# Audio-tower kernel: the instruction lists of all engines laid out anew, pair-2 convolution taps and weight centring moved to TensorE

## The reference, cut to what matters

```python
x_sp = depthwise conv over tokens, 3 taps, padding 1, + conv_b
h    = x_sp.T @ lin_w.T + lin_b + emb.mean(0)          # 250 x 128
h    = layernorm(h) * ln_g + ln_b
n    = layernorm(h)
QK   = (n Wq) (n Wk)^T                                 # 250 x 250
c0   = argmin(row sums of QK of batch 0)
A    = softmax(QK / 8), row c0 set to zero
h    = h + A (n Wv)
n    = layernorm(h)
h    = h + tril(W2) gelu(tril(W1) n + b1) + b2         # along the 128 features
```

## Time and profile before

| what | value |
|---|---|
| time, median of three runs | 105.33 us (104.79 to 105.63) |
| the profiled execution: its own time | 105.14 us |
| the profiled execution: its span, first to last instruction | 102.7 us |
| busy share of the span | TensorE 88%, VectorE 74%, ScalarE 69%, GpSimd 45% |
| granted TensorE clock, mean | 0.996 |

### The profile page before, as it was taken

The page is one execution under the profiler, slowest core; times in us unless marked ns, Lnnn a source line. Parts: engine busy times, 40 slices in busy tenths (PEclk is TensorE's granted clock), DMA queues, the critical chain, the costliest instruction groups (busy, mean ns, idle before and its releaser), DMA issues.

```text
span 102.7 us, 1986 instructions
## 1 busy us (share of the span) xinstructions
PE 90.9 (88%) x568; PEld 74.5 (73%) x568; DVE 76.2 (74%) x297; ACT 70.8 (69%) x219; POOL 46.4 (45%) x68
## 2 busy tenths in 40 slices
PE   5999769986926999999999997999999989999960
PEld 2356358865915998998998996998899758887750
DVE  2437999984479999898996996569778789943450
ACT  2747969969577996897897949874764983664310
POOL 6008562674727408918919909263071181900000
PEclk9999999999999999999999999999999999999998
DMA  2993000000000000000000000000000000345445
GB/s 35 199 301 118 0 0 3 3 0 6 0 0 0 0 0 0 0 6 0 0 6 3 0 6 0 0 0 0 0 0 6 0 0 0 95 135 144 124 127 172
DMA packets 3971, 3.83 MB, mean 37 GB/s; under 512 B 429, under 2 KB 3962, under 8 KB 3962
## 3 DMA queue, kind: packets, MB, share of 16 engines
q1 hardware_dynamic: 3610, 3.35, 11.6%
q10 hardware_dynamic: 352, 0.38, 1.4%
HBM read 1.68 MB, written 2.05 MB: 36 GB/s over the span
## 4 chain that ended last, share of the span: by engine, by line
PE 59%; DVE 14%; ACT 12%; POOL 6%; issue 5%; ACTq 0%; POOLq 0%; DVEq 0%
PE bank_o L414 10%; PE bank_s L389 10%; PE bank_s L443 6%; PE bank_pv L321 5%; PE bank_pv L369 5%; POOL root_all L265 4%; PE bank_pv L374 4%; PE bank_x L427 3%; PE bank_nt L438 3%; PE bank_at L401 3%; ACT squared L541 3%; PE bank_pv L438 2%; DVE neg_max L754 2%; ACT a L583 2%; DVE bn L742 2%
## 5 line engine op out<-in xcount | busy, mean ns | idle before, releaser
L389 PE MATMUL bank_s<-n1t,pv 128*125 128x250 f32 x64 | 16.9, 387 | 3.8 <-ACT pv L576 3.7
L583 ACT ACTIVATE a<-bank_s,neg_max 125x250 f32<-125x250 f32 x32 | 13.2, 468 | 7.5 <-DVE neg_max L754 7.5
L414 PE MATMUL bank_o<-pv,at_sb 125*125 125x129 f32 x128 | 16.9, 273 | 0.4 <-DVE h_all L764 0.4
L414 PEld LDWEIGHTS bank_o<-pv,at_sb 125*125 125x125 f32 x128 | 15.4, 187 | 1.1 <-ACT at_sb L591 1.1
L265 POOL TENSOR_TENSOR root_all<-ve_all,neg_half 125x4 f32<-125x4 f32 (+2 forms) x10 | 15.9, 1585 | 0.8
L389 PEld LDWEIGHTS bank_s<-n1t,pv 128*125 128x125 f32 x64 | 11.2, 187 | 6.3 <-ACT pv L576 5.1
L262 POOL TENSOR_TENSOR ve_all<-mv_all,eps 125x4 f32<-125x4 f32 (+2 forms) x10 | 2.4, 242 | 29.1 <-DVE mv_all L749 14.6
L754 DVE TENSOR_REDUCE neg_max<-bank_s 125x2 f32<-125x500 f32 x16 | 10.7, 667 | 1.8 <-PE bank_s L389 1.7
L561 ACT ACTIVATE n<-h_all,root_all 125x128 f32<-125x128 f32 x24 | 8.4, 405 | 4.7 <-POOL root_all L265 4.7
L369 PE MATMUL bank_pv<-n1t,qk_w 128*128 128x250 f32 x32 | 9.9, 391 | 1.2 <-ACT n1t L632 0.7
L764 DVE SCALAR_TENSOR_TENSOR h_all<-bank_o,rinv_keep,h_all 125x128 f32<-125x128 f32 x32 | 9.8, 347 | 0.6
(11 more groups left out here) (132 smaller groups left out, 185.3 us busy)
## 6 DMA issues: line engine op xcount, KB each, us to landing
out_dram<-hb_all SPq DMA_DIRECT2D x7, 224.0 KB
x_all<-x_dram SPq DMA_DIRECT2D x8, 125.0 KB, 4.8
out_dram<-hb_all SPq DMA_DIRECT2D x2, 112.0 KB
w_sb<-weights_dram SPq DMA_DIRECT2D x1, 192.0 KB, 5.4
rows_sb<-rows_dram ACTq DMA_DIRECT2D x1, 187.5 KB
out_dram<-hb_all SPq DMA_DIRECT2D x6, 26.0 KB
tok_w<-tok_dram ACTq DMA_DIRECT2D x1, 130.0 KB, 3.0
w_sb<-weights_dram SPq DMA_DIRECT2D x1, 128.5 KB, 5.0
```

Source lines behind the costliest of these rows:

```text
L389: last = nc.tensor.matmul(s_ps[b % 2][:, a, :], p_sb(b)[:, a * H:(a + 1) * H], n1t[b % 2][:, :], start=True, stop=True)
L414: last = nc.tensor.matmul(o_ps[:, a, 0:DV], at_sb[:, c, a * H:(a + 1) * H], v_sb(b, c), start=(c == 0), stop=(c == 1))
L583: last = nc.scalar.activation(a_sb[b % 2][:, a, :], s_ps[b % 2][:, a, :], ACT.Exp, bias=neg_max[b % 2][:, a:a + 1])
```

## The change

It changes what is computed where, and the order of all lists.

- **Lists.** The regular loops of TensorE, ScalarE and VectorE are replaced by flat lists with another order. GpSimd's loop is replaced as well.
- **By batch.** `scale_x`, `squares`, `moments_1`, `gather_1`, `gather_2` work on one batch (two tiles) rather than a pair, each with its own semaphore count. `project` is split into `project_bias` and two `project_half`.
- **Second moments apart.** `shared_root(i)` no longer holds the second moments: it has 8 columns at most. They get calls of their own, `second_root`, three for two pairs each (8 columns) and two for one pair (4 columns).
- **Weight centring on TensorE.** The raw Wq and Wk are multiplied, and the 128x128 product is multiplied twice with the centring matrix `cen`; ScalarE copies after each (`out_qk`, three copies). The accumulator and bias passes (L619, L623) are gone.
- **Pair 2.** Its three taps are made apart by ScalarE (`product`), and TensorE sums them: six `project_half` rather than two. VectorE's two taps of pair 2 are gone.
- **Small.** The five later filler matmuls are gone. Projections use other banks. The `w1`, `w2` masks on GpSimd come later. One VectorE step of the bias row's split is gone.

```diff
         def x_bank(k):
-            return bank_o if k == 2 else bank_x[k % 2]
+            return bank_o if k == 3 else bank_x[(1, 1, 0, 0, 1, 0, 1, 0)[k]]
...
             def shared_root(i):
-                lo, hi = 12, 0
+                lo = 4
                 if i + 3 < NP:
-                    pool.wait_ge(xvar_ready, pair_count(i + 3))
-                    lo, hi = 0, 4
-                if i + 2 < NP:
-                    pool.wait_ge(stats1, stats1_count(i + 2))
-                    lo, hi = min(lo, 4), 8
-                if i >= 2:
-                    pool.wait_ge(stats2, i - 1)
-                    lo, hi = min(lo, 8), 12
+                    pool.wait_ge(xvar_ready, 2 * i + 8)
+                    lo = 0
+                pool.wait_ge(stats1, 2 * i + 6)
...
+            def second_root(turn, first, count):
+                cols = slice(4 * first, 4 * (first + count))
+                pool.wait_ge(stats2, 2 * (first + count))
...
+            def project_half(k, a, tap=0):
+                if k == 2:
+                    pe.wait_ge(prod_ready, tap + 1)
+                    rows = prod[tap][:, :]
+                else:
+                    pe.wait_ge(conv_ready, k + 1 if k < 2 else k)
+                    rows = xc[:, k, :]
...
+            def qk_centre(n):
+                pe.wait_ge(cen_ready, 1)
+                pe.wait_ge(qk_step, n + 1)
+                nc.tensor.matmul(bank_s[1][:, (n + 1) * D:(n + 2) * D], (qk_raw, qk_half)[n][:, :], cen[:, :],
+                                 start=True, stop=True).then_inc(qk_mm, 1)
...
-            keep_warm(5)
...
+            def product(i):
+                act.wait_ge(landed_x[2], 16)
+                act.wait_ge(pads_zeroed, 2)
+                if i == 0:
+                    last = nc.scalar.activation(prod[0][:, :], x_all[:, 2, 0:T], ACT.Identity, bias=conv_b, scale=taps[0])
+                else:
+                    last = nc.scalar.activation(prod[i][:, :], x_all[:, 2, i:i + T], ACT.Copy, scale=taps[i])
+                last.then_inc(prod_ready, 1)
```

More of the change, by code:

```diff
@@ L488, in _ @@
+            project_bias(5)
+            turn_n1(3)
+            project_half(5, 0)
             turn_a(0)
[L489 to L503 removed]
@@ L504, in _ @@
-            scores(NB - 2)
-            queries(NB - 1)
-            values(NB - 1).then_inc(pv_mm, 1)
-            attend(NB - 4)
-            turn_a(NB - 3)
+            scores(2)
+            turn_n1(4)
+            queries(3)
+            project_half(5, 1)
+            values(3)
+            attend(0)
+            turn_a(1)
+            scores(3)
+            queries(4)
+            values(4)
+            turn_n1(5)
+            attend(1)
+            scores(4)
+            turn_a(2)
+            queries(5)
@@ new lines, in _ @@
+            turn_n1(6)
+            values(5)
+            turn_a(3)
+            attend(2)
+            scores(5)
+            queries(6)
+            values(6)
+            turn_n1(7)
+            attend(3)
+            scores(6)
+            turn_a(4)
+            queries(7)
+            values(7)
+            project_bias(6)
+            turn_n1(8)
+            project_half(6, 0)
+            turn_a(5)
+            project_half(6, 1)
+            scores(7)
+            attend(4)
+            queries(8)
@@ new lines, in _ @@
+            values(8)
+            project_bias(7)
+            turn_n1(9)
+            project_half(7, 0)
+            project_half(7, 1)
+            scores(8)
+            attend(5)
+            turn_a(6)
+            queries(9)
+            values(9)
+            turn_n1(10)
+            turn_a(7)
+            attend(6)
+            scores(9)
+            queries(10)
+            values(10)
+            turn_n1(11)
+            attend(7)
+            scores(10)
+            w1_centre()
+            turn_a(8)
@@ new lines, in _ @@
+            turn_n1(12)
+            queries(11)
+            values(11)
+            turn_a(9)
+            attend(8)
+            scores(11)
+            turn_n1(13)
+            queries(12)
+            values(12)
+            turn_a(10)
+            attend(9)
+            scores(12)
+            queries(13)
+            values(13)
+            attend(10)
+            turn_n1(14)
+            scores(13)
+            turn_a(11)
+            turn_n1(15)
+            queries(14)
+            values(14)
@@ L509, in _ @@
+            attend(11)
+            turn_a(12)
+            scores(14)
+            queries(15)
+            values(15)
+            attend(12)
+            turn_a(13)
             turn_n2(0)
-            scores(NB - 1)
+            scores(15)
             turn_n2(1)
-            attend(NB - 3)
-            turn_a(NB - 2)
+            attend(13)
+            turn_a(14)
+            turn_n2(2)
             up(0)
-            turn_n2(2)
-            turn_a(NB - 1)
-            attend(NB - 2)
+            attend(14)
@@ L656, in _ @@
             normalize_1(4)
[L657 to L677 removed]
+            normalize_1(5)
```

848 lines of the change are left out of this document (543 added, 305 removed).

## The result

| | before | changed |
|---|---|---|
| median us (runs) | 105.3 (4) | 95.52 (4) |
| lowest to highest | 104.79 to 105.63 | 95.27 to 95.87 |
| ratio, 95% interval | 1 | 0.9077, 0.9025 to 0.913 |
| profiled execution, span | 105.14, 102.7 | 95.76, 94.0 |

The direction was right and the size short. The ratios leave out executions that took over 1.5% more than the fastest of their kernel.

A forecast was written before the change was run, and what follows sets the result against it. TensorE was taken as the bound, idling 5.97 us in the head and working nearly throughout afterwards. 105.14 - 5.1 (head) - 1.75 (second part) = 98.3, stated as 98.4 us; range 95.8 to 101.6.

The forecast's parts named there:

- The walk: Head, from 8.34 us: new lists followed instruction by instruction with steps from rows; claimed a gain of 6.1 us.
- Some 20 hops lie on this path, so I take off 0.05 each: 5.1 us kept.: Head: allowance for hops between engines longer than assumed, cutting the gain from 6.1 to 5.1 us.
- I take half, 1.75 us: Second part, 39.50 to 98.20 us: the new order recovers half of 3.5 us of waits.
- the batch 8 row maximum behind twelve VectorE steps: Second part, VectorE's list: a late row maximum named as speaking against full recovery of the 3.5 us; no size of its own.
- full walk and full recovery: Whole kernel: lower bound with 6.1 us gained in the head and 3.5 in the second part, 95.5 us.
- one serial round of a pair, with an unrelated batch queued behind it: Head, scores of batch 3 after 3.05 us idle: batch 2's row maximum queued behind pair 3's round through GpSimd.
- At nothing: Parts priced at zero: more root calls, ScalarE's product passes against centring passes, loads of x, the tail after 98.2 us.
- The added half products: Head: four more projection halves for pair 2 on TensorE, 0.43 us each, 1.72 us of added work.
- VectorE as the bound: Between 28 and 54 us VectorE's list needs 26.3 us against TensorE's 23.6; 100.8 or 101 us, chance 12%.
- The long wait at later pairs: Late GpSimd semaphores hold row maxima again, 3.05 us each; about 104.5 us at 5%, 107 at 7%.
- The clock: Head: without five fillers TensorE's clock could dip, costing 2 us, so 100.4 us; chance 3%.

The follow-up runs named there:

- a_fill: Changed kernel with the five later filler matmuls back ahead of the first transpose; median 96.11 us, ratio to before 0.9135.
- a_dve: Changed kernel with twelve more VectorE operations (4.6 us), results unread, spread over the second part; median 96.59 us, ratio to before 0.9117.
- b_max: Kernel before with VectorE's row maximum of batch 2 moved ahead of the moments of pair 3; median 103.62 us, ratio 0.9881.
- a_taps: Changed kernel with pair 2's taps on ScalarE and VectorE again, two projection halves rather than six; median 96.33 us, ratio to before 0.9205.
- a_regular: Changed kernel with its new head, then before's regular order on TensorE, ScalarE and VectorE; median 101.14 us, ratio to before 0.9596.
- a_dvereg: Changed kernel with only VectorE's list back in before's regular order behind the head; median 98.88 us, ratio to before 0.9387.
- a_pereg: Changed kernel with only TensorE's list back in before's regular order behind attend of batch 1; median 105.13 us, ratio to before 0.9999.
- b_nofill: Kernel before without its five later fillers, nothing in their place; median 106.46 us, ratio 1.0074.
- a_same: The changed kernel run again unaltered, as the measure for others on the same chip; median 95.18 us, ratio to before 0.9055.

## Why the prediction was right or wrong

**The walk was right nearly to the tenth.** The profile of the changed kernel begins 0.33 us late; with that added, the forecast starts and the rows are: first transpose 14.63 and 14.64, scores 0 17.08 and 16.97, scores 3 27.28 and 27.20, scores 5 33.73 and 33.76. The first row maximum came at 20.60 (forecast 20.5 plus 0.33), from the mark 3.0 us later than before, with no TensorE idle behind it. The first shared root ends at 23.04, forecast 22.8 plus 0.33. The walked gain of 6.1 us is 6.07.

**Step that failed: "Some 20 hops lie on this path, so I take off 0.05 each: 5.1 us kept."** This term of 1.0 us should have been none: 6.07 us were kept. The walk already had its hops of 0.05 to 0.1 in it, and its TensorE start times were met to 0.11 us or better without a further allowance. In the new head TensorE has no recorded wait (23.51 of 23.51 busy), so hops of the other engines lie beside its work; in a_fill, TensorE work added there shows as 0.98 of 1.08.

**Step that failed: "I take half, 1.75 us"** of the 3.5 us of waits in the second part. 3.17 came back. The work of 55.2 us was right (54.48 us measured to the last downs, plus the 1.05 by which 98.20 lies behind their start, is 55.53). So the term is 1.4 us too low: a half was taken where nearly all of it was to be had. What I set against it, the batch 8 row maximum behind twelve VectorE steps, opened no wait on TensorE. a_dve fits that, since 4.6 us more of VectorE's work cost only 1.31. Why the new lists leave none of these waits is shown only so far as that old lists bring them back.

**The range cut off its own bound.** By the prediction's own line, full walk and full recovery give 95.5, and the range began at 95.8. The median is 95.52: both terms came out near their upper bound.

**The remaining 0.5 us.** These two steps are 2.4 of the 2.9 us missed. The profiled execution moved by 105.14 - 95.76 = 9.38 (forecast 6.85), of which 9.24 are the length, -0.33 the late begin, -0.21 the tail inside the span (5.55 and 5.76 us behind the start of the last downs) and +0.68 what lies outside the span (2.44 and 1.76 us). This last part says nothing of the change: over the other executions of before it varies from 1.76 to 2.79. The rest is that this execution is 0.24 over its median and that I rounded up by 0.1.

**The reason "one serial round of a pair, with an unrelated batch queued behind it" was right, but is one link of several.** b_max takes the queueing out and gets 0.79 us; ScalarE's list holds the next wait. In the changed kernel the root comes 3.67 us earlier (14.18 for 17.85), and the lists behind it fit: put before's lists behind the new head and 5.05 of 9.24 us are lost again, put TensorE's alone and all is.

**"At nothing"** held: tail and outputs 0.2 us; centring 0.03. The added half products, priced at 1.72 for TensorE, are not paid for: without them a_taps is 0.94 longer, in part by the place of one tap.

**The rivals.** VectorE as the bound: fallen (a_dve). The long wait at later pairs: absent, with no recorded TensorE idle; but a_regular, a_dvereg and a_pereg each open waits with a list that fits less well (1.22, 1.69 and 1.31 us as the longest). In the first two it is the forecast's chain from a row maximum behind moments (ScalarE's exponentials wait 0.61 and 1.76 us for it), though there VectorE is held by its own queue and not by GpSimd; in a_pereg it is a residual. The clock: 1.00 in both stretches here. b_nofill shows that the fall I weighed exists, and that "no run here shows a fall later" no longer holds. The Trainium skill ("TensorE: Matmul & The Clock Gate", section "What's actually happening") says that idling throttles the clock and sustained work releases it; b_nofill agrees behind its 3.04 us wait; its first fall goes further, since TensorE was not idle throughout but busy 1.23 of 3.00 us, and the measurement decides. The changed kernel has no recorded pause between 8.34 and 89.50 us behind which this could happen. That may be a gain of its own: in the experiments' comparisons 33 of 54 executions of before have a mean granted clock of 0.968 to 0.984, with spans 0.6 to 1.1 us longer (medians by chip) than the others; the four of b_max, whose wait is shorter, have 0.997 or more. No trace of such an execution was kept, so where its clock falls, and whether the long wait is the reason, is not shown.

**Not settled.** How the head's 6.07 us divide. Tested alone, the taps give 0.94 (with the place of one), the fillers 0.98, the centring 0.03, the second-moment roots in before 0.18. The largest share is by exclusion the lists of the head with scaling by batch, which is argued and not shown: the two were not tried apart.

## What to carry to other kernels

When in-order lists wait for each other, walk the new lists instruction by instruction with durations from rows; then trust the walk, take nothing further off for hops that lie beside a full engine, and let the range reach as far as the terms' own bounds. A reordering is worth what all lists together give: one edit on one list got 0.79 us of a 3.05 us wait, and one list out of step lost the whole gain, so follow a wait to the next list before you price its removal. Work may go to the busiest engine where, at that moment, another one is late. When you put a part back to test it, look where its new place makes an engine wait, or the place is measured with it.

## What was not expected of the hardware

The mark moves by 0.84 us between executions of one program. The first rows of TensorE in the changed kernel and in a_same, the same program:

```profile
6.18 1.11 PE L418 MATMUL bank_x<-lin_blk,xc 64*125 64x128 f32 x4
```

```profile
5.72 0.73 PE L418 MATMUL bank_x<-lin_blk,xc 64*125 64x128 f32 x4
6.38 0.43 PE L378 MATMUL bank_s<-emb_c,mean_w 128*65 128x128 f32 x2
```

The same four products take 1.11 and 0.73 us, and the bias-row product starts at 7.22 and 6.38. The rows have no wait before them, so the rate of TensorE rises at another moment; this is read from the durations, as the granted clock of the page is 1.00 here in both, and also while the nine fillers take 0.45 us each. Behind it the two traces agree within 0.02 us up to the last downs (81.02 both). Comparing traces from such a mark rather than from the span's start is what made effects of 0.03 to 0.3 us readable.
